# One Trainium2 core, an embedding, attention and MoE tower: the q and k projection as three F32R products, and output tile 0 moved ahead of the last heads

## The reference

```python
h = tok(x)                                  # hot rows from a table, cold rows as latent @ proj.T
h = h + attn(layernorm(h))                  # 16 heads of 32, causal softmax, output projection w_out
h = h + ffn(layernorm(h))                   # top 2 of 16 experts (512 -> 256 -> 512, SiLU gate) + a shared expert

qkv = einsum('bsd,od->bso', x, w_project)   # what the change touches: q and k out of this
att = einsum('bhqd,bhkd->bhqk', q, k) / sqrt(32)
out = einsum('bhqk,bhkd->bhqd', softmax(causal(att)), v)
return einsum('bsd,od->bso', out, w_out)    # and this, for its first tile of 128 tokens
```

## Time and profile before

| | |
|---|---|
| median of 3 runs | 1009.49 us (1009.37 to 1011.67) |
| the profiled execution | 1011.66 us |
| span of its trace | 1009.9 us |
| busy: PE / weight loads / DVE / ACT / POOL | 936.1 / 683.8 / 661.0 / 602.1 / 311.0 us |
| granted TensorE clock, mean | 0.97 of full speed; 1.00 from 130 to 620 us |
| chain that ended last, by engine | PE 73%, DVE 10%, DMA 6%, ACT 3% |

### The profile page before, as it was taken

The page is one execution under the profiler, slowest core; times in us unless marked ns, Lnnn a source line. Parts: engine busy times, 40 slices in busy tenths (PEclk is TensorE's granted clock), DMA queues, the critical chain, the costliest instruction groups (busy, mean ns, idle before and its releaser), DMA issues.

```text
span 1009.9 us, 21200 instructions
## 1 busy us (share of the span) xinstructions
PE 936.1 (93%) x6811; PEld 683.8 (68%) x6811; DVE 661.0 (65%) x1748; ACT 602.1 (60%) x1308; POOL 311.0 (31%) x312
## 2 busy tenths in 40 slices
PE   6679899999999999999997989899989999999992
PEld 5335568686776858778685678777866677766660
DVE  8885567575666756566575767658867666666660
ACT  7212477776777777676778822221147777777770
POOL 2276220201102020110202016433254477356441
PEclk9689899999999999999999999999989999999996
DMA  6135454340623324051336021261449678846633
GB/s 221 38 95 128 129 112 116 77 93 3 135 65 84 85 63 107 34 127 42 84 85 212 1 105 64 67 277 44 176 152 385 160 132 184 264 85 121 94 44 42
DMA packets 46111, 114.40 MB, mean 113 GB/s; under 512 B 9844, under 2 KB 11892, under 8 KB 43698
## 3 DMA queue, kind: packets, MB, share of 16 engines
q1 hardware_dynamic: 33682, 87.14, 29.3%
q0 software_dynamic: 12320, 25.90, 14.1%
HBM read 53.03 MB, written 25.17 MB: 77 GB/s over the span
## 4 chain that ended last, share of the span: by engine, by line
PE 73%; DVE 10%; DMA 6%; issue 5%; ACT 3%; POOL 1%; POOLq 1%; DVEq 0%; ACTq 0%
PE psum L609 12%; PE psum L570 10%; PE psum L1438 9%; PE psum L622 7%; PE psum L599 7%; DMA out<-xnT,slot_out 6%; PE psum L1513 5%; PE psum L575 5%; PE psum L1378 5%; PE psum L1362 3%; PE psum L1460 2%; PE psum L625 2%; PE psum L1482 2%; DVE oh_lo L1673 1%; DVE oh_hi L1671 1%
## 5 line engine op out<-in xcount | busy, mean ns | idle before, releaser
L699 ACT ACTIVATE probs<-psum,nmax 128x128 f32<-128x128 f32 (+7 forms) x256 | 190.8, 746 | 39.2 <-DVE nmax L741 33.0
L741 DVE CUSTOM_DVE_ANT_0 psum<-psum,mask_row 128x128 f32<-128x128 f32 (+7 forms) x256 | 192.0, 768 | 27.2 <-PE psum L599 25.4
L609 PE MATMUL psum<-ident,probs 128*128 128x128 f32 x1152 | 173.7, 276 | 10.2 <-ACT probs L699 4.1
L609 PEld LDWEIGHTS psum<-ident,probs 128*128 128x128 f32 x1152 | 134.8, 140 | 55.6 <-ACT probs L699 19.6
L599 PE MATMUL psum<-k_stack,q_stack 128*128 128x512 f32 (+2 forms) x384 | 155.3, 464 | 3.8 <-ACT probs L699 2.5
L684 ACT COPY probsT<-psum 128x512 f32<-128x512 f32 (+3 forms) x256 | 129.0, 504 | 38.0 <-PE psum L609 33.3
L570 PE MATMUL psum<-xnT,w_unit 128*128 128x512 f32 x256 | 130.8, 600 | 0.4 <-issue 0.2
L466 POOL CAST part_hi<-full 128x512 fp32r<-128x512 f32 x28 | 17.2, 613 | 339.8 <-ACT full L494 233.5
L967 POOL DMA_INDIRECT out<-xnT,slot_out x47 | 83.0, 1767 | 105.5 <-DMA out<-xnT,slot_out 73.3
L756 DVE TENSOR_TENSOR attnT<-psum,z_rows 128x128 f32<-128x128 f32 x64 | 18.7, 292 | 132.2 <-ACT z_rows L706 132.2
L599 PEld LDWEIGHTS psum<-k_stack,q_stack 128*128 128x128 f32 x384 | 68.2, 202 | 35.7 <-issue 20.2
(11 more groups left out here) (248 smaller groups left out, 1848.6 us busy)
## 6 DMA issues: line engine op xcount, KB each, us to landing
w_gu<-in_wgu SPq DMA_DIRECT2D x16, 1024.0 KB, 7.2
w_dn<-in_wd SPq DMA_DIRECT2D x16, 512.0 KB, 8.9
q_stack<-part_hi SPq DMA_DIRECT2D x56, 128.0 KB, 2.4
q_stack<-part_lo SPq DMA_DIRECT2D x56, 128.0 KB, 2.4
k_stack<-part_hi SPq DMA_DIRECT2D x56, 128.0 KB, 2.4
k_stack<-part_lo SPq DMA_DIRECT2D x56, 128.0 KB, 2.4
out<-acc SPq DMA_DIRECT2D x17, 256.0 KB, 2.7
hot_all<-xn SPq DMA_DIRECT2D x4, 1024.0 KB, 8.1
```

Source lines behind the costliest of these rows:

```text
L609: mm = pe.transpose(bank(4 + m % 2)[:, (j - 4 * k) * P:(j - 4 * k + 1) * P], probs[n % PSLOTS][:, j * P:(j + 1) * P], ident[:, :])
L699: act.activation(probs[n % PSLOTS][:, 0:(i + 1) * P], score_bank(n)[:, 0:(i + 1) * P], ACT.Exp, bias=nmax[:, n % 4:n % 4 + 1], scale=-1.0, ...
L741: dve.tensor_tensor_reduce(out=row, in0=row, in1=mask_row[:, (QT - 1 - i) * P:QT * P], scale=1.0, scalar=3.0e38, op0=ALU.add, op1=ALU.min, ...
```

## The change

Five edits, all in attention and at its end:

1. The q and k pieces of units 1 to 7 are three F32R products each instead of one float32 product: high weights by low rows, high by high, low weights by high rows. POOL makes the parts: `wq_hi`, `wq_lo` of the weights (4 parts of 256 columns, once per head group) and `x_hi`, `x_lo` of `xnT` (4 parts of 512 columns per half, so 8 a unit). There is one buffer for a half's rows: part c of the second half is made when the first half's q and k products of part c are done.
2. The fills go q, k of the first half, q, k of the second, then v, since q and k of a half share the row parts. ACT copies out the q fills (n = 6 and 16), DVE the k fills (n = 11 and 21). Unit 0's projection keeps its float32 products and its order.
3. To make room there is one q stack instead of two, and one k stack for the second 512 keys (`k_high`); only that for the first 512 keys is doubled (`k_low`). So the second half of a unit's stacks can only be loaded when the unit before has issued its last scores, and the stacks are loaded by halves: 64 DMAs of 32x512 a unit instead of 32 of 32x1024. PE waits for the second half (`s_high`) at score 16.
4. The weights are loaded by column part: q and k columns (`load_wq`) as soon as POOL has split those of the group before, a unit ahead; v columns (`load_wv`) when the last v fill is done, ahead of the second half of the stacks on SP's queue.
5. Output tile 0 is worked by PE between `turn(last, 31)` and `heads(last, 7)`. POOL splits the attention rows of tiles 0 and 1 during unit 7; ACT and DVE split tiles 2 to 15 as before. The semaphores of the h loads are shared by four tiles.

In the head, POOL splits the weights of group 0 inside the gather loop (tiles 9 to 12) and the first row part between the last `rstd` operations.

```diff
+        def stack_half(sp, u, side, half):
+            b = u % 2
+            sp.wait_ge(s_lo, HEAD + 4 * u + 2 * half + side + 1)
+            for r in range(4):
+                low = r % 2 if side == 0 else r // 2
+                src = part_lo if low else part_hi
                 for h in range(GH):
-                    sp.dma_start(st[32 * r:32 * r + 32, h, :].bitcast(F32), ...
+                    if side == 0:
+                        dst = q_stack[32 * r:32 * r + 32, h, half * 512:half * 512 + 512]
+                    else:
+                        dst = (k_high if half else k_low[b])[32 * r:32 * r + 32, h, :]
+                    sp.dma_start(dst.bitcast(F32), ...).then_inc((s_high if half else s_low)[b], 16)

         def att_sp(sp):
-            def group(g, last):
-                stack(sp, 2 * g + 1, 1)
-                if not last:
-                    sp.wait_ge(s_fill, HEAD + 2 * FILLS * (g + 1))
-                    load_w(sp, g + 1)
-                    stack(sp, 2 * g + 2, 0)
+            for u in range(1, 2 * GROUPS):
+                if u % 2 and u < 2 * GROUPS - 1:
+                    sp.wait_ge(s_wqlo, KC * (u // 2 + 1))
+                    load_wq(sp, u // 2 + 1)
+                sp.wait_ge(s_S, HEAD + (u - 1) * STEPS + NARROW)
+                for side in range(2):
+                    stack_half(sp, u, side, 0)
+                if u % 2 and u < 2 * GROUPS - 1:
+                    sp.wait_ge(s_fill, HEAD + FILLS * (u + 1))
+                    load_wv(sp, u // 2 + 1)
+                sp.wait_ge(s_S, HEAD + u * STEPS)
+                for side in range(2):
+                    stack_half(sp, u, side, 1)

+        def split_rows_in(pool, u, half, c, part="both"):
+            ...
+                v, p = (u, 1) if half else (u - 1, 3)
+                if c < KC - 1:
+                    pool.wait_ge(s_xpused, 6 * (u - 1) + 3 * half - 3 + c + 1)
+                else:
+                    pool.wait_ge(s_fill, HEAD + FILLS * v + p + 1)
+            ...
+                pool.tensor_copy(x_hi[:, c, :], src).then_inc(s_xphi, 1)
+            ...
+            pool.tensor_tensor(x_lo[:, c, :], src, x_hi[:, c, :].bitcast(F32), ALU.subtract).then_inc(s_xplo, 1)

         def att_pool(pool):
+            for u in range(1, 2 * GROUPS):
+                for c in range(KC):
+                    if u % 2 == 0:
+                        split_weights_in(pool, u, c)
+                    if u > 1 or c > 0:
+                        split_rows_in(pool, u, 0, c)
+                split_part(pool, u, 0, 0)
+                for c in range(KC):
+                    split_rows_in(pool, u, 1, c)
+                split_part(pool, u, 1, 0)
+                split_part(pool, u, 0, 1)
+                split_part(pool, u, 1, 1)

         def fill_piece(pe, u, b, f, k, loads):
...
+                side, half = f % 2, f // 2
+                if side == 0:
+                    pe.wait_ge(s_wqlo, 4 * (u // 2) + k + 1)
+                    pe.wait_ge(s_xplo, 8 * (u - 1) + 4 * half + k + 1)
+                for t, (w, x) in enumerate(((wq_hi, x_lo), (wq_hi, x_hi), (wq_lo, x_hi))):
+                    mm = pe.matmul(bank(7), w[:, k, side * P:(side + 1) * P], x[:, k, :], ...)

         scores:
+                if n == NARROW:
+                    pe.wait_ge(s_high[b], STACKED * (u // 2 + 1))

         att_pe, at the end:
             turn(last, STEPS - 1)
+            pe.wait_ge(s_wolo, KC)
+            output_tile(pe, 0)
             heads(last, 1, QT - 1)
```

More of the change, by code:

```diff
@@ L553, in first_piece @@
             for k in range(KC):
-                fill_products(pe, 0, f, k)
+                if f < 4:
+                    side, half = f % 2, f // 2
+                    mm = pe.matmul(bank(7), w_unit[:, k, side * P:(side + 1) * P],
+                                   xnT[:, k, half * 512:half * 512 + 512],
+                                   start=(k == 0), stop=(k == KC - 1), skip_group_check=True)
+                else:
+                    mm = value_products(pe, 0, f, k)
+            mm.then_inc(s_fill, 1)
@@ L577, in fill_products, with value_products, output_tile @@
             if k == KC - 1:
                 mm.then_inc(s_fill, 1)
+        def value_products(pe, b, f, k):
+            t0 = b * SEQ + ((f - 4) * 4 + k) * P
+            for c in range(KC):
+                mm = pe.matmul(bank(7)[:, k * P:(k + 1) * P], xnT[:, c, t0:t0 + P],
+                               w_unit[:, c, 2 * P:3 * P], start=(c == 0), stop=(c == KC - 1))
+            return mm
+        def output_tile(pe, c):
+            pe.wait_ge(s_atlo, c + 1)
+            for g in range(GROUPS):
+                for t, (x, w) in enumerate(((at_hi, wo_hi), (at_lo, wo_hi), (at_hi, wo_lo))):
+                    mm = pe.matmul(bank(c % 2), x[:, c % 2, g * P:(g + 1) * P], w[:, g, :],
+                                   start=(g == 0 and t == 0), stop=(g == GROUPS - 1 and t == 2))
+            mm.then_inc(s_op, 1)
```

218 lines of the change are left out of this document (111 added, 107 removed).

## The result

The changed kernel takes 994.69 us in the median of 4 runs (993.92 to 995.51) against 1010.22 of the kernel before on the same chip, a ratio of 0.9849 [0.9834, 0.9864], 15.5 us less. The forecast was 992 with a range of 984 to 1001. A later group of 4 runs gave 995.79 (995.51 to 996.58), ratio 0.9856 [0.9841, 0.9872].

What follows compares the result with a forecast made beforehand. PE was taken to bound units 0 to 6. Products -17.9, stack waits +2.4, VectorE behind POOL +1.0 and the end -2.8 sum to -17.3 us, from the 1009.49 median to 992 us, range 984 to 1001.

Steps and rivals of the forecast that it cites:

- The products: q and k pieces on PE, units 1 to 7: three F32R products take 0.69 us against 0.86, 17.9 us less in all.
- from first start to the next scores: Sign to look for on PE's timeline: triples in 0.69 us, measured between these two points.
- 15 pieces x 0.17: Gain per attention unit: 15 of 16 pieces each give back 0.17 us, 2.6 us a unit.
- so the loop stays hidden: Scores, maximum, exponential, turn and copies stay behind PE: stretches of 5.5 and 7.2 us against unit 7's 5.00 and 6.41.
- A term that I left at zero: One ScalarE q copy moves to n = 16, where ScalarE was on the chain; no time charged, the loss left to a rival.
- Stack waits: PE at score 16 of units 1, 3, 5 waits 0.8 us each for the second stack batch: +2.4 us.
- counts as even: Unit 7 has no v load, so its second stack batch was treated like the even units', which do not wait.
- VectorE behind POOL: VectorE's L750 copies held by POOL's splits, four or five of a unit's eight: 0.15 us a unit, +1.0 in all.
- The end: End of attention: tile 0 fills PE's wait before the heads, tile 2 starts near 588.2 instead of 591.1: -2.8 us.
- Open loads: Rival: weight loads of each triple are not hidden, a piece costs 0.88 us; about 1010, half open about 1000; chance 0.10.
- SP as the bound: Rival: SP's queue of stack DMAs bounds, at 0.79 us an issue, slower than before, about 1015 us; chance 0.06.
- ScalarE and VectorE as the bound: Rival: these engines become the bound in attention, half of each unit's 2.6 us is lost, about 999 us; chance 0.12.

## Why the prediction was right, and where it was not

**What bounds.** Right: PE does, in units 0 to 6, and shorter pieces shorten the unit.

**The products,** -17.9 us forecast. A triple takes 0.69 to 0.70, as read from the earlier trace rows, though not "from first start to the next scores", which is 0.78 since the first record starts early. The three loads lie hidden. The page "TensorE: Matmul & The Clock Gate" (Part 3, what overlaps and what doesn't) of the Trainium skill is contradicted once more. The sum failed at "15 pieces x 0.17": measured are 1.7 us a unit, 12 in seven units, that is ten pieces' worth. The step that failed is "so the loop stays hidden": for heads x16 to x24 and x24 to x32 I had 5.5 and 7.2, and the rows after give 5.90 (357.63 to 363.53) and 7.21. The 7.21 is right by luck. The kernel with the order of the pieces alone takes 7.37 there, so 0.34 of the 0.50 us come from the order and only 0.16 from the products. The first stretch stood against unit 7's 5.00, but unit 7 has no copies out of bank 7, so it is no floor for a unit that has them. And the stretch has VectorE's copy behind POOL in it, which I priced apart and spread as a mean. I gave the loop a rival and charged the forecast nothing; it happened to a quarter of the pieces.

**A term that I left at zero** made up for half of that. I saw that ScalarE gets the copy at step 16 and feared a loss. I did not ask what VectorE, which had it before, was holding up: 0.34 us a unit, 2.4 in all. Another 1.2 us in unit 0 and step 12 were not foreseen, and they are not all the change's: unit 0 begins in a stretch at half clock, which covers its first 3.9 us before and its first 2.8 after. With the products that is 12.1 + 2.4 + 1.2 = 15.7 of the 17.9.

**Stack waits,** +2.4 forecast: the mechanism is right, at score 16 behind k's low parts, with issues at 0.63. The v weights took 0.60 us to issue where I had 0.35. Measured are 1.9 us in the one trace and 1.0 in the other (+0.7 and +0.85 in units 1 and 3, +0.3 in unit 7; then 0.2 and 0.8). Wrong was that unit 7 "counts as even": its steps 2 to 15 carry no pieces, so the same batch has 2.6 us less cover there (17.4 against 20.0 us from the first exponential to step 15). Unit 5 had none in either trace. And of the 20 issues of the earlier trace rows I called 12 at or below 0.70; by the rows it is 16 (5.63 for 8 is 0.704).

**VectorE behind POOL,** +1.0: the mechanism is right, its place is not, and the size is right by luck. I spread it over the units and let VectorE's idle time absorb most. 19 of the 64 copies are long instead of 13, not four or five in each eight, and the median is still 0.227 us as in the earlier trace rows. In units 0 to 6 those at steps 8 and 24 cost nothing (steps 24 and 25 of unit 4 together last 3.82 us before and after). That at step 12 is on the path and ends in the 0.2 us for which PE idles, at most some 1.4 us in seven units by my estimate; it stands in the loss of the products above. In unit 7 another 1.0 us is lost, because the splits of `wo`, which ran early in it, now come late (POOL's first `wo` cast at 538.71), next to steps 20 and 24. I had written that these splits end well before step 31 and not asked what they run beside.

**The end,** -2.8 forecast, -2.7 measured, tile 2 at 8.1 us behind the last blocks' end. The size is right by its two ends; which of the two edits earns it was wrong, as shown. The blocks' end was misread too: 579.84 is where the chain turns off to ScalarE, the last block ends at 580.31, and PE waits 0.83 us there and not 1.3.

**Rivals.** Open loads and SP as the bound fell with the first trace. ScalarE and VectorE as the bound is true for 4 of 16 pieces here, and for most at two products.

**The median** is 2.7 us above the forecast. 0.7 of it is the median of the kernel before, 1010.22 with a fourth run and not 1009.49. 1.8 is the drop, 15.5 us for the 17.3 of the sum. The first trace has the same 15.5: 15.7 - 1.9 - 1.0 + 2.7. The rest is rounding. The close agreement can be chance; the later group's drop is 14.6.

## What to carry to other kernels

A stage without the work is a floor for the stage with it only if everything that the work brings along to other engines is counted too; compare stretch by stretch, and expect a cut to be paid only where the bounding engine has no rival within the size of the cut. An operation that another engine holds grows when it starts earlier, and can eat such a cut. When a step moves from one engine to another, price what it gave back on the first as well as what it costs on the second. A batch of DMA issues that just fits is late at random, and first in the unit whose other work is lightest; and splitting ahead of a dependent stage was worth more than filling the gap in front of it.

## What the runs showed that was not expected

- 64 KB stack DMAs issue at 0.63 us, as those of 128 KB did; single ones of the same form take 1 us more.
- A 128x128 reciprocal takes 0.947 us, four times the 0.227 of the copy and 5.6 times the 0.17 of a 128x4 reciprocal.
